# Last attention's scores: from fp32 matmuls to three fp32r passes, with keys and queries split into a high and a low part

## The reference

```python
Q = (layernorm(x) @ Wq + bq).reshape(B, S, 8, 4, 16).transpose(0, 2, 3, 1, 4)
K = (ctx @ Wk + bk).reshape(B, S, 8, 16).transpose(0, 2, 1, 3)
V = (ctx @ Wv + bv).reshape(B, S, 8, 16).transpose(0, 2, 1, 3)
scores = jnp.einsum('bhgqd,bhkd->bhgqk', Q, K) / sqrt(16)
y = jnp.einsum('bhgqk,bhkd->bhgqd', softmax(scores), V)
x = x + tanh(g_xattn[3]) * (y.transpose(0, 3, 1, 2, 4).reshape(B, S, 512) @ Wo + bo)
```

## Time and profile before

| | before |
|---|---|
| median of 3 runs | 1615.02 us (1611.8 to 1615.87) |
| the profiled execution | 1614.25 us, span 1612.5 us, so 1.75 us lie outside the span |
| PE busy | 1570.8 us (97%) |
| DVE busy | 977.4 us (61%) |
| ACT busy | 741.2 us (46%) |
| POOL busy | 399.8 us (25%) |
| mean granted PE clock | 0.997 |

### The profile page before, as it was taken

The page is one execution under the profiler, slowest core; times in us unless marked ns, Lnnn a source line. Parts: engine busy times, 40 slices in busy tenths (PEclk is TensorE's granted clock), DMA queues, the critical chain, the costliest instruction groups (busy, mean ns, idle before and its releaser), DMA issues.

```text
span 1612.5 us, 25907 instructions
## 1 busy us (share of the span) xinstructions
PE 1570.8 (97%) x8958; PEld 1262.4 (78%) x8958; DVE 977.4 (61%) x2629; ACT 741.2 (46%) x2151; POOL 399.8 (25%) x278
## 2 busy tenths in 40 slices
PE   8999999999999999999999999999999999999987
PEld 7788888888888888888885877868696788666556
DVE  6762663626636356364686774848476767756677
ACT  5442443424434344243432462735355332288873
POOL 3131321313203132032203300000001343377651
PEclk9999999999999999999999999999999999999999
DMA  5110111101111011111224000000001613000001
GB/s 180 53 43 30 56 42 52 42 29 55 42 52 42 29 55 42 39 43 43 79 80 195 14 1 14 0 13 0 0 1 41 223 53 108 14 14 15 1 1 53
DMA packets 34435, 76.22 MB, mean 47 GB/s; under 512 B 5568, under 2 KB 18496, under 8 KB 32192
## 3 DMA queue, kind: packets, MB, share of 16 engines
q1 hardware_dynamic: 34368, 75.36, 14.0%
HBM read 73.25 MB, written 2.10 MB: 47 GB/s over the span
## 4 chain that ended last, share of the span: by engine, by line
PE 78%; DVE 11%; ACT 4%; issue 3%; DVEq 2%; POOL 1%; DMA 1%; POOLq 0%; SPq 0%; ACTq 0%
PE banks L1197 10%; PE banks L1142 10%; PE banks L1115 10%; PE banks L1123 9%; PE banks L1357 9%; PE banks L1461 5%; PE banks L1254 3%; PE banks L1237 3%; PE banks L1433 3%; PE banks L1244 2%; ACT p L992 2%; PE banks L1564 1%; PE banks L1571 1%; PE banks L1587 1%; PE banks L1381 1%
## 5 line engine op out<-in xcount | busy, mean ns | idle before, releaser
L1197 PE MATMUL banks<-w_o,atT 128*128 128x512 f32 x720 | 181.0, 397 | 0.0
L535 POOL TENSOR_TENSOR w_q<-w_raw_q,w_q 128x1792 fp32r<-128x1792 f32 x15 | 61.1, 4072 | 479.6 <-ACT w_q L741 479.6
L1115 PE MATMUL banks<-cT,w_k 128*128 128x512 f32 x720 | 178.0, 396 | 0.0
L1142 PE MATMUL banks<-w_v,cT 128*128 128x512 f32 x768 | 176.5, 390 | 0.0
L1142 PEld LDWEIGHTS banks<-w_v,cT 128*128 128x128 f32 x768 | 144.0, 188 | 29.7
L1123 PE MATMUL banks<-xT,w_q 128*128 128x512 f32 x672 | 164.0, 395 | 0.7 <-ACT kT L731 0.7
L1898 DVE TENSOR_TENSOR sA<-banks,pbias 128x512 f32<-128x512 f32 x62 | 42.8, 690 | 186.5 <-PE banks L1237 185.7
L1115 PEld LDWEIGHTS banks<-cT,w_k 128*128 128x128 f32 x720 | 132.0, 188 | 25.4
L1197 PEld LDWEIGHTS banks<-w_o,atT 128*128 128x128 f32 x720 | 131.8, 188 | 25.4
L1123 PEld LDWEIGHTS banks<-xT,w_q 128*128 128x128 f32 x672 | 123.8, 188 | 26.0 <-ACT kT L731 1.1
L800 ACT ACTIVATE sA<-sA,nmA 128x128 f32<-128x128 f32 x248 | 96.4, 393 | 55.8 <-DVE nmA L1903 55.5
(11 more groups left out here) (291 smaller groups left out, 3275.3 us busy)
## 6 DMA issues: line engine op xcount, KB each, us to landing
w_raw_v<-in_w0v SPq DMA_DIRECT2D x8, 1024.0 KB, 4.8
w_raw_q<-in_w0q SPq DMA_DIRECT2D x16, 512.0 KB, 3.3
w_raw_k<-in_w0k SPq DMA_DIRECT2D x15, 512.0 KB, 3.4
w_raw_o<-in_w0o SPq DMA_DIRECT2D x15, 512.0 KB, 3.3
cTp<-in_ctxT SPq DMA_DIRECT2D x12, 512.0 KB, 3.9
wq_raw<-in_wq SPq DMA_DIRECT2D x1, 3072.0 KB, 10.0
wo<-in_wo SPq DMA_DIRECT2D x1, 3072.0 KB, 20.3
x_res<-in_x SPq DMA_DIRECT2D x4, 512.0 KB, 11.4
```

Of the source, the lines that this page charges most:

```text
L535: pool.tensor_tensor(w_part[slot][1][:], w_raw[slot][:], w_part[slot][0][:].bitcast(F32), ALU.subtract).then_inc(S(f"w{slot}_lo"), 1)
L1115: mm = pe.matmul(dst, wk_[l][:, c, h * P:(h + 1) * P], cT[r][:, c, half * HT:(half + 1) * HT], start=c == 0 and n == 0, stop=c == DC - 1 a ...
L1142: mm = pe.matmul(dst, cT[l][:, c, b * P:(b + 1) * P], wv_[r][:, c, :], start=n == 0, stop=n == 3 * DC - 1)
L1197: mm = pe.matmul(dst, at_at(l, p, b // 4 * 2 + h)[:, t], w[r][:, h, :], start=start and n == 0, stop=stop and n == 5)
```

## The change

The scores become three fp32r matmuls for each half, high x high, high x low and low x high, accumulated in the same bank. For that the keys and the queries are needed in two parts.

- Keys: `keys` now reads the product out of PSUM twice, with 256 columns each (high part, then what is left), into `k3`, with a drain behind each. `keys_of(i, j)` expands one batch's part of both into `kbd` and `kbd_part1`: two tensor_tensor instructions of 128x512 for each batch, both inputs in SBUF. The expansion of the second batch stands one unit later.
- Queries: ACT writes the high part; `queries_lo` on DVE makes the low part from PSUM and the high part, two instructions of 128x256 for two groups. PE's waits on `q3_ready` become waits on `q_lo`.
- The scale of the scores moves into `kmask`, so DVE's small instruction on `bq3` falls away. `q3_lo`, `k3` and `kbd_lo` lie over buffers that are not yet in use.

```diff
@@ scores on PE
-                    for half in range(2):
-                        rows = slice(half * HALF3, (half + 1) * HALF3)
-                        if U > 1:
-                            pe.wait_ge(S("x3_e"), 2 * (U - 2) + half + 1)
-                        pe.matmul(banks2[2 - U % 2][:, half, :], q3[rows, i % 2, g, j * P:(j + 1) * P], kbd[rows, i % 2, j],
-                                  start=True, stop=True).then_inc(S("x3_s"), 1)
+                    if U == 1:
+                        pe.wait_ge(S("kv3_ready"), 5)
+                    elif g == 0:
+                        pe.wait_ge(S("kv3_ready"), 5 * i + 2 + j)
                     if g % 2 == 0 and j == 0:
-                        pe.wait_ge(S("q3_ready"), 2 * i + g // 2 + 1)
+                        pe.wait_ge(S("q_lo"), Q_LO_1 + 2 * i + g // 2 + 1)
+                    if U > 1:
+                        pe.wait_ge(S("x3_e"), 2 * (U - 2) + 2)
+                    for n, (l, r) in enumerate(PASSES):
+                        for half in range(2):
+                            rows = slice(half * HALF3, (half + 1) * HALF3)
+                            mm = pe.matmul(banks2[2 - U % 2][:, half, :], (q3, q3_lo)[l][rows, i % 2, g, j * P:(j + 1) * P],
+                                           (kbd, kbd_lo)[r][rows, i % 2, j], start=n == 0, stop=n == len(PASSES) - 1)
+                            if n == len(PASSES) - 1:
+                                mm.then_inc(S("x3_s"), 1)
@@ x3_dve
-                    for j in range(2):
-                        dve.scalar_tensor_tensor(out=kbd[:, i % 2, j], in0=bank(6)[:, j * P:(j + 1) * P].unsqueeze(1)
-                                                 .to_broadcast([P, KV3 // 2, P]),
-                                                 scalar=bk3[:, 0:1], in1=kmask2[:].unsqueeze(2).to_broadcast([P, KV3 // 2, P]),
-                                                 op0=ALU.add, op1=ALU.mult).then_inc(S("kv3_ready"), 1)
+                    src = bank(6)[:, 0:PT2]
+                    dve.tensor_scalar(k3[0][:].bitcast(F32R), src, bk3[:, 0:1], None, ALU.add)
+                    dve.drain()
+                    dve.scalar_tensor_tensor(out=k3[1][:], in0=src, scalar=bk3[:, 0:1], in1=k3[0][:], op0=ALU.add,
+                                             op1=ALU.subtract).then_inc(S("kv3_ready"), 1)
+                    dve.drain()
+                def keys_of(i, j):
+                    for l, dst in enumerate((kbd, kbd_lo)):
+                        e = dve.tensor_tensor(dst[:, i % 2, j],
+                                              k3[l][:, j * P:(j + 1) * P].unsqueeze(1).to_broadcast([P, KV3 // 2, P]),
+                                              kmask2[:].unsqueeze(2).to_broadcast([P, KV3 // 2, P]), ALU.mult)
+                    e.then_inc(S("kv3_ready"), 1)
+                def queries_lo(i, g0, b):
+                    dve.wait_ge(S("q3_ready"), 2 * i + g0 // 2 + 1)
+                    for g in (g0, g0 + 1):
+                        e = dve.scalar_tensor_tensor(out=q3_lo[:, i % 2, g, :], in0=bank(b)[:, (g % 2) * PT2:(g % 2 + 1) * PT2],
+                                                     scalar=bq3[:, g:g + 1], in1=q3[:, i % 2, g, :].bitcast(F32), op0=ALU.add,
+                                                     op1=ALU.subtract)
+                    e.then_inc(S("q_lo"), 1)
...
                 keys(0)
+                keys_of(0, 0)
+                queries_lo(0, 0, 7)
+                keys_of(0, 1)
                 values(0)
                 ln_stats(2)
                 row_max(0, 0)
...
                 row_max(1, 1)
+                queries_lo(0, 2, 6)
                 sums(0, 1)
...
                     if u == G3:
                         attended(i, 0)
+                        if i + 1 < NPAIR:
+                            queries_lo(i + 1, 2, 7)
...
+                    if i + 1 < NPAIR and u == (2 if i == 0 else 1):
+                        queries_lo(i + 1, 0, 7)
```

More of the change, by code:

```diff
@@ L61 @@
 PARTS = {L1X: 0, L1F: 1, L2X: 2, L2F: 3}
+Q_LO_1 = 2 * KV1 * NPAIR
 BUSY = 13
@@ L229, in build @@
         xs = sb(ctx_b, "xs", [P, 2, 2, D])
+        ctx_g = ExitStack()
+        q3_lo = sb(ctx_g, "q3_part1", [P, 2, G3, PT2], F32R)
+        ctx_g.close()
         qTs = sb(ctx_b, "qTs", [P, 2, DC, PT2], F32R)
         wd3_hi = sb(ctx_b, "wd3_0", [P, IC3, D], F32R)
+        ctx_g = ExitStack()
+        k3 = [sb(ctx_g, f"k3_{l}", [P, PT2]) for l in range(2)]
+        ctx_g.close()
         eg = sb(ctx_b, "eg", [P, 2, I3])
@@ L335, in build @@
         kmask2 = sb(ctx_p, "kmask2", [P, KV3 // 2])
-        kbd = sb(ctx_p, "kbd", [P, 2, 2, KV3 // 2, P])
-        q3 = sb(ctx_p, "q3", [P, 2, G3, PT2])
+        kbd = sb(ctx_p, "kbd", [P, 2, 2, KV3 // 2, P], F32R)
+        q3 = sb(ctx_p, "q3", [P, 2, G3, PT2], F32R)
         p3 = sb(ctx_p, "p3", [P, 3, KV3, P])
@@ L344, in build @@
         rsc = sb(ctx_p, "rsc", [P, 2, 2])
+        ctx_g = ExitStack()
+        kbd_lo = sb(ctx_g, "kbd_part1", [P, 2, 2, KV3 // 2, P], F32R)
+        ctx_g.close()
         sg = sb(ctx_p, "sg", [P, 2, I3])
@@ L348, in build @@
         iq = sb(ctx_p, "iq", [P, 2, I3])
+        iT = sb(ctx_p, "iT", [P, 2, IC3, P], F32R)
         ami = sb(ctx_p, "ami", [P, 2])
@@ L647, in _ @@
             pool.wait_ge(S("res"), NB * (L2X + 1))
-            pool.memset(kmask[:], 1.0)
+            pool.memset(kmask[:], float(HD3) ** -0.5)
             pool.memset(vbd[:], 0.0)
@@ L983, in queries @@
                         e = act.activation(q3[:, i % 2, g, :], bank(b)[:, (g % 2) * PT2:(g % 2 + 1) * PT2], ACT.Identity,
-                                           bias=bq3[:, g:g + 1], scale=float(HD3) ** -0.5)
+                                           bias=bq3[:, g:g + 1])
                     e.then_inc(S("q3_ready"), 1)
@@ L1078, in _ @@
             pairs_ahead(act, lambda i, last: store_next(L2F, i, last))
-            act.wait_ge(S("scaled"), 3)
+            act.wait_ge(S("x3_ld"), 7 * 16)
             x3_act()
             def round_inner(i):
-                act.wait_ge(S("scaled"), (4, 6, 7)[i])
+                act.wait_ge(S("scaled"), (3, 5, 6)[i])
                 for j in range(2):
@@ L1087, in round_rows @@
             def round_rows():
-                act.wait_ge(S("scaled"), 5)
+                act.wait_ge(S("scaled"), 4)
                 for j in range(2):
@@ L1599, in attend @@
                     if U % U3 == 0:
-                        pe.wait_ge(S("kv3_ready"), 4 * i + 4)
+                        pe.wait_ge(S("kv3_ready"), 5 * i + 5)
                     if U % U3 == G3 and i + 1 < NPAIR:
-                        pe.wait_ge(S("q3_ready"), 2 * i + 4)
+                        pe.wait_ge(S("q_lo"), Q_LO_1 + 2 * i + 4)
                     elif U % U3 == G3:
@@ L1652, in x3_pe @@
                 x3_queries(0, 0, 2, 7)
-                pe.wait_ge(S("kv3_ready"), 4)
+                pe.wait_ge(S("kv3_ready"), 1)
                 x3_queries(0, 2, 3, 6)
@@ L2277, in first_pair @@
                         keys(1)
+                        keys_of(1, 0)
                     if u == 5:
                         next_apply(L3X, 1)
+                        keys_of(1, 1)
                     if u == 6:
@@ L2302, in middle_pair @@
                         keys(i + 1)
+                        keys_of(i + 1, 0)
                     if u == 5:
+                        keys_of(i + 1, 1)
                         if i + 2 < NPAIR:
```

14 lines of the change are left out of this document (5 added, 9 removed).

## The result

The changed kernel takes 1624.38 us (median of 4 runs, 1622.24 to 1625.04) against 1614.08 us (4 runs, 1611.8 to 1615.87): 1.0063 times the time before, 95% interval 1.005 to 1.0075. It is slower, by about 10 us. The forecast was 1626, from 1617 to 1634, with 0.80 on slower.

The account below looks back on a forecast made before the run. Bound by ACT at the head, PE from 1417 to 1500, then no full engine, with a DVE-ACT ring passing delays on; 2.4 + 0.1 + 4.7 + 4.2 = +11.4 us gave 1626 us, range 1617 to 1634.

Parts of the forecast that it names:

- The head: Start of the last attention: DVE's low part of the queries waits for ACT's copies, delaying the first row maximum 2.4 us.
- The second low part at the head: Behind `row_max(1,1)`: delays unit 2's scores by 0.8 us more, priced at nothing, at most 0.8.
- the cover: At the head: ACT still has the second unit's exponentials while unit 2's scores are late; failure costs up to 0.8 us.
- PE's clock at the head: PE's clock rate at the head; the prediction as given here states no claim or size for it.
- PE's scores: Each unit's scores take 0.90 us, saving 0.16; 2.6 us where PE is the chain, 5.1 at most.
- The rival of halves one after the other: fp32r row halves not side by side: 1.6 us per unit's scores, 1628 to 1636 us in all; chance 0.10.
- the ring's terms: Pairs 0 to 2: DVE's row maxima and ACT's exponentials wait on each other, passing on DVE's added work; +0.1 and +4.7.
- Pairs 0 to 2: DVE's added key and query work delays the row maxima: net +0.1 us in pair 0, +4.7 in pairs 1 and 2.
- the shared time: Pairs 1 to 3: 12 DVE expansions with both inputs in SBUF slow beside POOL, 0.35 us each, +4.2.
- The shape of pair 1: Unit 1: low part waits for ACT's copies, statistics follow, row maximum some 2.0 us late; +2.5 for the pair.
- The tail: End of the program: the last pair and the feed-forward take as long as before.
- a delay on both sides: Two-SBUF-input DVE and SBUF-reading POOL instructions exclude each other; POOL's divisions would slow too, sum nearer 14 than 11 us.

Follow-up runs that it names:

- e3: Changed kernel with the low part of the first queries moved behind the second expansion, values and statistics at the head; 1621.6 us, ratio 1.0045.
- e5: Changed kernel without the low part of the queries, the third pass using the high part again; 1617.01 us, ratio 1.0019 to the kernel before.
- e4: Changed kernel with 18 unused identity matmuls in PE's gap at the head, ahead of unit 2's scores; 1622.36 us, ratio 1.0048.
- e1: Kernel before with PE's part alone: three fp32r passes over the same high parts, no low parts; 1611.65 us against 1614.61, ratio 0.9978.
- e2: Changed kernel with all its DVE work, but scores in one fp32 pass over the high parts; 1623.7 us against 1614.61, ratio 1.0058.
- e8: e7 with the low keys expanded by POOL and the high keys by DVE straight from PSUM; 1617.31 us, ratio 1.0018.
- e7: e3 plus, in pairs 0 to 2, the low part of the next pair's queries moved behind the statistics; 1618.16 us, ratio 1.0029.
- e9: e8 plus the 18 filler matmuls of e4 in PE's gap at the head; ratio 1.0022.
- e10: e9 plus the second low part of each pair's queries moved behind the row maximum in unit 4; ratio 1.0021.
- e6: Changed kernel without the low part of the keys, one expansion per batch, second pass using the high part again; 1619.27 us, ratio 1.0028.

## Why the prediction was right, and where its terms were off

- **The head, +2.4.** Measured 2.3, with the low part, an expansion, the values and the statistics between, as it said. e3 and e5 show the cause: with the low part behind the statistics, or without it, the shift is 0.1 and -0.2.
- **The second low part at the head, priced at nothing, "up to 0.8" if the cover fails.** The cover held. The scores of unit 2 came 0.9 us later still, but in e4, at full clock, `turn(2)` is only 2.1 us late behind scores that are 3.2 late, and in e3 it is not late at all behind scores that are 1.1 late.
- **PE's clock at the head, named and left without a price.** This is the term that was missed. PE, having stood for 4.04 us, worked on at half clock, and `turn(2)` was 3.5 us late in place of 2.1: 1.3 us, by e4 against after.
- **PE's scores.** Forecast 0.90 us for a unit, measured 0.89 in the chain. The rival of halves one after the other, 1.6 us, is refuted: in after a pair of records takes 0.23 us from start to start (1428.20 to 1428.43). The Trainium skill (TensorEngine Tiling (Array Packing), section Tiling Modes) has tiles working in parallel; the trace now agrees for fp32r as well. The saving is 0.17 us in each unit and 3.0 us in e1 up to `turn(23)`, but only 0.7 us separate the profiles of after and e2, and their medians do not show even that (ratios 1.0063 and 1.0058): it was rightly inside the ring's terms and not beside them.
- **Pairs 0 to 2, +0.1 and +4.7, and the shared time, +4.2.** In all 9.0 forecast; measured 0.7, 3.1 and 2.0, 5.8 in all. The last is read at the row maximum of unit 31: before and after both have a half-clock stretch ahead of it, and at `turn(23)` only 0.5 of it is to be seen. So this part was sized 3.2 us too high. DVE's expansions did grow beside POOL as foreseen, and the groups by line of after give the amount:

```profile
L2255 DVE TENSOR_TENSOR kbd<-k,kmask 128x512 fp32r<-128x512 f32 x8 | 7.5, 939 | 0.4
L2255 DVE TENSOR_TENSOR kbd_part<-k,kmask 128x512 fp32r<-128x512 f32 x8 | 7.1, 891 | 0.0
```

  Against 0.69 us alone that is 8 x 0.25 + 8 x 0.20 = 3.6 us of DVE time, near the 4.2. What failed is that I let all of it pass to the end on top of the ring's own delays: the two terms together are more than what came. e8, where DVE's expansions read one operand from PSUM, and e7 differ too little to say how much of the 3.6 us was ever felt; that stays open.
- **The shape of pair 1.** The prediction's mechanism, the low part's wait for ACT with the statistics stranded behind, is there: e7 takes 1.3 of the 3.1 us away by order alone, and e5 1.9 by leaving the low part out.
- **The tail.** Forecast as before; measured +0.2. PE's idle time in the middle, 6.5 us, also came as forecast (some 5 us or more).

The sum was 11.4; the profiles show 9.5 from the last attention's start, and the medians 10.3. The direction and the head are right by their mechanism. That the total came so near is in part luck: two errors of opposite sign, 1.3 us for the clock that I did not price, and 3.2 us too much for the ring and POOL.

## What to carry to other kernels

An instruction that waits for another engine's copy should stand behind everything in its queue that is ready: here moving one such step at the head (two instructions) behind the statistics was worth some 3 us by the ratios (1.0063 to 1.0045), nearly a third of the loss, and 3.6 us by the profiles, with the same work. A shorter step on one engine and a longer one on another do not add when the two take turns in a ring; each part has to be measured in the presence of the other. When a change makes TensorE wait for some us, price the clock behind the wait as well. And a difference of 1 to 2 us between two single profiles may be a stretch at half clock and not the edit: look for the stretches of both before reading it.

## What the runs showed of the hardware

- **PE after a gap.** After 4.04 us of waiting PE's clock fell to the lower level and cost 1.3 us; with matmuls of no use in the gap it stayed at the upper one (e4, e9, e10). The length of the gap alone does not decide it. The three longest gaps ahead of the scores of unit 2 (after 4.04, e6 4.03, e2 3.87 us) are all followed by a stretch at half clock. Of the three of 2.7 us only e8's is (0.66 in 1410 to 1415), and e3's and e7's are not; of the three of 1.6 to 1.8 us only e5's is, and not before's and e1's. The rows are those of PE in e3 and in e5:

```profile
1409.47 0.50 PE L1602 MATMUL banks<-kbd,q 64*128 64x512 f32 x2 [2.70 <-DVE q_part L2263]
```

```profile
1409.25 0.50 PE L1602 MATMUL banks<-kbd,q 64*128 64x512 f32 x2 [1.81 <-ACT q L994]
```

  In e8 `turn(2)` was 1.0 us later than in e3. In e5 the stretch at 1410.2 cost nothing that can be seen: the chain there is ACT's from 1405.57 to 1417.22.
- **A half-clock stretch in the last pair comes and goes** between kernels that differ elsewhere: it is in the profiles of before, after, e2, e3, e9 and e10, and not in the other six. In before it is this window:

```profile
1546.00:1549.00 3.00, 1.27 (x10) 0.79 (x8) 2.77 (x7) 2.57 (x12) 1.79 (x2) 1.00 0.00 0
1549.00:1554.00 5.00, 4.89 (x28) 2.03 (x29) 2.01 (x6) 2.90 (x16) 5.00 (x6) 0.66 0.00 0
```

  PE had been idle for over half of the 3 us ahead of it. But e1, without such a stretch, has idle time of the same kind there: PE is busy for 5.69 of the 9 us from 1542 to 1551, at a clock of 1.00. The six kernels without it all have the stretch near 41 us; of the six with it only after has that one too. The runs of before, one kernel with mean clocks from 0.995 to 1.000, show that such stretches differ between executions with no change of the program, so the column cannot be put down to the edits; what decides it is not settled. A stretch in the last pair is worth 1.4 to 1.5 us at the row maximum of unit 31 (e9 against e8, after against e4) and 0.6 to 0.7 at the end, as much as several of the effects studied, so a difference of 0.1% between two versions here says little about their order of instructions.
- **DVE and POOL.** The prediction expected, by the Trainium skill (SBUF — State Buffer, section Who interferes with whom), a delay on both sides. In after DVE's expansions rose from 0.69 to 0.92 us on average and to 1.5 at most, while POOL's 64 divisions stayed at 1.06 us. The high-part expansions of e8, which take one operand from PSUM, are the control. Beside the same divisions all eight took between 0.741 and 0.743 us, where the sixteen of after, with both inputs in SBUF, took 0.677 to 1.524. Their row in e8:

```profile
L2265 DVE SCALAR_TENSOR_TENSOR kbd<-banks,bk,kmask 128x512 fp32r<-128x512 f32 x8 | 5.6, 742 | 0.0
```

  Single divisions do pay, as at 1487. The timeline of DVE in after:

```profile
1487.59 1.52 DVE L2255 TENSOR_TENSOR kbd_part<-k,kmask 128x512 fp32r<-128x512 f32 x1
```

  And that of POOL:

```profile
1487.07 1.49 POOL L685 TENSOR_TENSOR p<-p,rs 128x512 f32<-128x512 f32 x1
```

  So both may lose in one encounter, but on average the loss was DVE's.
